# Banded attention stage rewritten, with the norm before it and the norm and gate after it moved inside

## The chip, the cores and the metric

One Trainium2 chip, one core. The metric is the device time of one execution in microseconds (us), median of the runs. The profile is of one execution of its own.

## The reference, cut to what matters

The model is attention A, an expert mixture, banded attention B, an expert mixture, each behind a layer norm and added to x (8 x 512 x 256, fp32). The change touches only this part:

```python
# x: (8, 512, 256)
x = x + attn_b(layernorm(x))          # 16 heads of 64, window 128, causal
h = layernorm(x)                      # goes on to the second mixture
scores = softmax(h @ gate_w.T)        # 16 experts
# attn_b:
q, k = rmsnorm(x @ wq.T) * q_gamma, rmsnorm(x @ wk.T) * k_gamma   # over all 1024 channels
v = x @ wv.T
s = q @ k.T / 8 + slope_h * (j - i);  s = -1e9 where j > i or j < i - 128
return (softmax(s) @ v) @ wo.T
```

## The kernel before

`hybrid_block` (L2439) runs stages one after the other; each ends on all engines before the next starts. Three stages stand where the change is made:

- `norm_stage` "n2" (L125): per batch of 512 tokens it loads x2, takes mean and variance (L373, L377, L379), POOL raises to the power -1/2 (L349), DVE normalizes (L387), PE transposes (L278), ACT copies (L324), and SP writes the transposed rows `xnT` to DRAM.
- `window_stage` "b" (L1217): 32 tiles of 128 tokens (NT = 4 per batch, B = 8). It reads `xnT` back and writes x3 = x2 + attention.
- `norm_stage` "n3": the same norm on x3, which also writes `xn` and `xnT`, and the gate: logits on PE (L290), softmax over 16 experts into `scores` (L395 to L400).

Inside `window_stage` one round does the attention of tile (b, t), the projections of the next tile and the output projection of the tile before. `WINDOW_ORDER` (L1205) is the order written out by hand that PE and DVE follow; ACT follows nearly the same (`WINDOW_SCALAR_ORDER`). Its steps:

- **Sections** share the one PSUM bank `ps_w`, and each waits until the one before is emptied. `q`, `k`, `v` (two halves each, L1403): six matmuls, 512 wide, with both operands split in a high and a rest part (fp32r, three products for two chunks of channels). q and k are emptied in two steps: ACT squares the bank with a running sum (L1482), then DVE multiplies it by gamma (L1553). v, `q_T`, `k_T` (transposes, L1410) and `out_T` (transposes of the attention output, L1415) are emptied by ACT copies. `out` (L1418): eight plain fp32 matmuls with `woT`, each of which PE runs as two instructions (so do all fp32 matmuls here that are no transposes), then the addition to x (L1560).
- `scores` k (0 to 3): four heads on PE, 64 rows each, two side by side (L1443); DVE adds the bias and takes the row's extreme (L1583); ACT takes exp with the row's sum (L1510).
- `probs_T` k (0 to 7): two heads' probabilities transposed (four transposes, L1452), copied by DVE (L1590).
- `values` k (0 to 7): two heads, the transposed probabilities as weights and v, 64 wide, moving (L1462). After four of them DVE divides by the row sums (L1595, L1596).

POOL does only the power for q and k (L1526) and the product with it (L1529). A tile with t = 0 has no band to its left, so its scores are 128 wide and its transposes and values are half as many. Batches 1 to 6 are a hardware loop (`Fori`, five ways back), the rest is written out. Before the first round DVE alone splits the weights (L445 to L447), in the same order of work as the emptying of the first sections.

Of the kernel before, what the change touches and what calls it, by code (L numbers as in the profile page):

```python
# [14 lines left out]
F32R = mybir.dt.float32r  # L15
# [1177 lines left out]
def scores_later(order, lags):  # L1193

    out = [x for x in order if x[0] != "scores"]
    for k, lag in enumerate(lags):
        place = sum(x[0] != "scores" for x in order[:order.index(("scores", k))]) + lag
        out.insert(min(place, len(order) - len(lags)) + k, ("scores", k))
    return out

WINDOW_ORDER = [  # L1205
    ("out_T", 0), ("scores", 0), ("out_T", 1), ("scores", 1), ("out", 0), ("probs_T", 0), ("probs_T", 1), ("q", 0),
    ("scores", 2), ("q", 1), ("values", 0), ("probs_T", 2), ("values", 1), ("probs_T", 3), ("k", 0),
    ("scores", 3), ("k", 1), ("values", 2), ("probs_T", 4), ("v", 0), ("values", 3), ("q_T", 0), ("probs_T", 5),
    ("q_T", 1), ("values", 4), ("probs_T", 6), ("values", 5), ("k_T", 0), ("probs_T", 7), ("values", 6), ("k_T", 1),
    ("values", 7), ("v", 1),  # L1210
]
WINDOW_SCALAR_ORDER = scores_later(WINDOW_ORDER, (1, 4, 4, 6))
NEXT = ("q", "k", "v", "q_T", "k_T")
PAST = ("out_T", "out")


def window_stage(nc, tag, const, x_d, xnT_d, wqT_d, wkT_d, wvT_d, woT_d, gamma_d, bias_d, y_d):  # L1217
# [9 lines left out]
    HW = BC // HALVES  # L1227
    with ExitStack() as ctx:
# [3 lines left out]
        woT = s.sb("woT", [P, CH, C])  # L1232
        gamma = s.sb("gamma", [P, 2, BC])
        bias = s.sb("bias", [P, BH, 2 * P])
        minus_half = s.sb("minus_half", [P, 2])
        xT = s.sb("xT", [P, 2, KC, P])
        xs = [s.sb(f"x_{part}", [P, 2, KC, P], F32R) for part in ("high", "rest")]
        masked = s.sb("masked", [P, HW])
        x = s.sb("x", [P, 2, C])
# [13 lines left out]
        score = s.sb("score", [P, 4, 2 * P])  # L1253
        low = s.sb("low", [P, 4])
        prob = s.sb("prob", [P, 4, 2 * P])
# [3 lines left out]
        o = s.sb("o", [P, 2, BC])  # L1259
        oT = s.sb("oT", [P, CH, P])  # L1260
# [5 lines left out]
        early_in = s.sem("early_in")  # L1266
        late_in = s.sem("late_in")
        xT_in = [s.sem(f"xT_in{p}") for p in range(2)]
        x_in = [s.sem(f"x_in{p}") for p in range(2)]
        y_out = [s.sem(f"y_out{p}") for p in range(2)]  # L1270
        chain = s.sem("chain")
        held = s.sem("held")
        half_set = s.sem("half_set")
        w_split = s.sem("w_split")
        x_split = s.sem("x_split")
        filled = s.sem("filled")
        emptied = s.sem("emptied")
        squared = s.sem("squared")
        ms_ready = s.sem("ms_ready")
# [4 lines left out]
        exped = s.sem("exped")  # L1284
        transposed = s.sem("transposed")
        copied = s.sem("copied")
        valued = s.sem("valued")
        o_taken = s.sem("o_taken")
        block = ctx.enter_context(s.programs())

        PROLOGUE = 10
        UNIT = 13

        def sections_before(b, t):
            return PROLOGUE if isinstance(b, int) and b == 0 and t == 0 else UNIT * (NT * b + t) + PROLOGUE - 3

        def steps(b, t, first, last, order=WINDOW_ORDER):

            n = sections_before(b, t)
            for kind, k in order:  # L1300
                if (kind in NEXT and last) or (kind in PAST and first):
                    continue
                yield kind, k, n
                if kind in NEXT or kind in PAST:
                    n = n + 1

        def units(engine, unit):

            for t in range(NT):
                unit(0, t, t == 0, False)  # L1310
            with engine.Fori(1, B - 1) as b:
                for t in range(NT):
                    unit(b, t, False, False)
            for t in range(NT):
                unit(B - 1, t, False, t == NT - 1)

        def following(b, t):
            return (b, t + 1) if t < NT - 1 else (b + 1, 0)

        def preceding(b, t):  # L1320
            return (b, t - 1) if t else (b - 1, NT - 1)

        def section_number(b, t, kind, k):

            early = isinstance(b, int) and b == 0 and t < 2
            place = [x for x in WINDOW_ORDER if x[0] in NEXT or (x[0] in PAST and not early)].index((kind, k))
            return place if early and t == 0 else sections_before(*preceding(b, t)) + place

        def first_tile():
            n = 0  # L1330
            for kind, k in WINDOW_ORDER:
                if kind in NEXT:
                    yield kind, k, n
                    n += 1

        def last_tile():
            n = sections_before(B - 1, NT - 1) + UNIT - PROLOGUE
            for kind, k in (("out_T", 0), ("out_T", 1), ("out", 0)):
                yield kind, k, n
                n += 1  # L1340

        def uses(b, t):

            return 2 * b + t // 2 + 1

        @block.sync
        def _(sp):
            def load_xT(b, t):
                sp.dma_start(xT[:, t % 2, :, :], xnT_d[ds(b, 1)].rearrange("a p k t -> p (a k) t")[:, :, t * P:(t + 1) * P]).then_inc(xT_in[t % 2], 16)

# [3 lines left out]
            def store(b, t, done):  # L1354

                hold(sp, emptied, done + 1, held)
                sp.dma_start(tokens(y_d, b, t), x[:, t % 2, :]).then_inc(y_out[t % 2], 16)

            def unit(b, t, first, last):
                static = isinstance(b, int)  # L1360

                if not (static and b == B - 1 and t >= 2):
                    hold(sp, emptied, sections_before(b, t), held)
                    load_xT(b + (t + 2) // NT, (t + 2) % NT)

                if not (static and b == 0 and t < 2):
                    past = (b, t - 2) if t >= 2 else (b - 1, t + 2)
                    store(*past, sections_before(*following(*past)) + 2)
                    hold(sp, y_out[t % 2], 16 * (uses(b, t) - 1), held)
                sp.dma_start(x[:, t % 2, :], tokens(x_d, b, t)).then_inc(x_in[t % 2], 16)  # L1370

            load_xT(0, 0)
            for tile, dram, sem in ((w_whole["q"], wqT_d, w_in["q"]), (ident, const["ident"], early_in), (gamma, gamma_d, early_in),
                                    (w_whole["k"], wkT_d, w_in["k"]), (w_whole["v"], wvT_d, w_in["v"]), (bias, bias_d, late_in), (woT, woT_d, late_in)):
                sp.dma_start(tile[tuple(slice(None) for _ in tile.shape)], dram).then_inc(sem, 16)
            load_xT(0, 1)
            units(nc.sync, unit)
            store(B - 1, NT - 2, sections_before(B - 1, NT - 1) + 2)
# [1219 lines left out]
```

## Time and profile before

| | |
|---|---|
| median of 3 runs | 4155.57 us (4155.28 to 4165.5) |
| the profiled execution, its own time | 4160.83 us |
| its span, first to last instruction | 4158.8 us |
| busy in the span | PE 88%, DVE 59%, ACT 44%, POOL 19% |
| mean granted TensorE clock | 0.946 |
| this part of the span | "n2" from 2118.7, "b" from 2168.9, "n3" 3285.4 to 3348.5 |

A busy PE is not PE at its peak: its matmuls overlap, so the distance from start to start tells their cost. A granted clock of 1.00 is 2.4 GHz, 0.50 is 1.2 GHz.

### The profile page before, as it was taken

Reading aid. Unit: us, or ns where it says so; the run is one execution under the profiler, and the core shown is the slowest. Engines: PE = TensorE matmul, PEld = TensorE weight load, DVE = VectorE, ACT = ScalarE, POOL = GpSimd, SP = SyncE. Lnnn points to the kernel's source line nnn. Section 1 sums busy time; section 2 is a strip of 40 time slices with the busy share of each in tenths; the row PEclk is TensorE's granted clock in tenths of the full one; section 3 lists DMA queues with packets and bytes.
Section 4 is the critical chain, followed back from the end, with each engine's and each line's share of the span. In section 5 each row is a group of like instructions: output and inputs, shape, how many; then the busy total and the mean of one; then the engine's idle time right before and its main releaser. Section 6 shows DMA issues by size and latency. Waiting matters only on the chain. (4 is left out here: it accounts for less than half of the span.)

```text
span 4158.8 us, 91975 instructions
## 1 busy us (share of the span) xinstructions
PE 3639.6 (88%) x33000; PEld 2872.0 (69%) x33000; DVE 2451.2 (59%) x5269; ACT 1842.3 (44%) x3752; POOL 780.7 (19%) x714
## 2 busy tenths in 40 slices
PE   4899999999966969999947899888989787899998
PEld 3566666666655858888835777777777676788887
DVE  4566666666645666666544545444545566666664
ACT  1466666666622324444413444444444232344443
POOL 0122222222210013333210000000000000233332
PEclk9999999999987979999969999999999788899999
DMA  4565556555534234333240000000000232343432
GB/s 178 145 172 170 174 172 173 168 171 174 169 123 150 86 119 122 110 108 117 75 142 33 13 13 12 13 13 13 13 13 15 87 118 93 117 122 111 115 110 44
DMA packets 383709, 424.97 MB, mean 102 GB/s; under 512 B 172864, under 2 KB 323008, under 8 KB 369728
## 3 DMA queue, kind: packets, MB, share of 16 engines
q1 hardware_dynamic: 358720, 386.04, 29.2%
q0 software_dynamic: 24576, 33.57, 4.6%
q8 instruction: 241, 3.95, 0.4%
q14 instruction: 172, 1.41, 0.1%
HBM read 269.24 MB, written 150.27 MB: 101 GB/s over the span
## 5 line engine op out<-in xcount | busy, mean ns | idle before, releaser
L2212 ACT ACTIVATE a_prob<-a_ps_s,a_low 128x512 f32<-128x512 f32 x512 | 318.9, 689 | 48.5 <-DVE a_low L2404 47.5
L2073 PE MATMUL a_ps_p<-a_ident,a_prob 128*128 128x128 f32 x2048 | 311.0, 285 | 14.9 <-ACT a_band L2192 9.0
L2404 DVE TENSOR_REDUCE a_low<-a_ps_s 128x2 f32<-128x1024 f32 x256 | 313.5, 1224 | 8.8
L2264 POOL TENSOR_TENSOR a_below<-a_probT,a_upper 128x512 f32<-128x512 f32 x128 | 164.3, 1284 | 726.4 <-ACT a_probT L2188 371.2
L2073 PEld LDWEIGHTS a_ps_p<-a_ident,a_prob 128*128 128x128 f32 x2048 | 217.7, 141 | 108.6 <-issue 83.3
L2188 ACT COPY a_probT<-a_ps_p 128x512 f32<-128x512 f32 x352 | 194.0, 588 | 155.6 <-PE a_ps_p L2073 155.6
L1510 ACT ACTIVATE b_prob<-b_score,b_low 128x256 f32<-128x256 f32 (+1 forms) x512 | 240.6, 473 | 23.7 <-PE b_ps_p L1452 23.7
L1462 PEld LDWEIGHTS b_ps_o<-b_v,b_probT 128*128 128x128 f32 x1792 | 227.2, 191 | 9.9 <-issue 0.9
L1583 DVE CUSTOM_DVE_ANT_0 b_score<-b_ps_s,b_bias 128x256 f32<-128x256 f32 (+1 forms) x512 | 186.0, 389 | 75.2 <-PE b_ps_s L1443 47.6
L1462 PE MATMUL b_ps_o<-b_v,b_probT 128*128 128x64 f32 x1792 | 228.2, 267 | 0.7 <-DVE b_o L1596 0.7
L2403 DVE TENSOR_TENSOR a_ps_s<-a_ps_s,a_win 128x320 f32<-128x320 f32 (+1 forms) x256 | 135.0, 527 | 140.2 <-PE a_ps_s L2106 135.7
L1590 DVE COPY b_probT<-b_ps_p 128x512 f32<-128x512 f32 (+1 forms) x256 | 155.7, 621 | 101.5 <-PE b_ps_p L1452 97.4
L1482 ACT ACTIVATE b_square<-b_ps_w 128x512 f32<-128x512 f32 x128 | 76.4, 597 | 298.5 <-PE b_ps_w L1403 298.5
L1526 POOL TENSOR_TENSOR b_rrms<-b_ms,b_minus_half 128x2 f32<-128x2 f32 x32 | 22.6, 707 | 972.5 <-DVE b_ms L1556 972.5
L490 ACT ACTIVATE ge_gelu<-ge_ps_g 128x512 f32<-128x512 f32 x128 | 76.5, 598 | 286.6 <-PE ge_ps_u L469 286.6
L490 ACT ACTIVATE fe_gelu<-fe_ps_g 128x512 f32<-128x512 f32 x128 | 76.5, 598 | 285.8 <-PE fe_ps_u L469 285.8
L903 POOL DMA_INDIRECT x<-fe_eo,fe_index_scatter x64 | 121.2, 1894 | 361.2 <-DVE fe_eo L1098 346.6
L903 POOL DMA_INDIRECT out<-ge_eo,ge_index_scatter x64 | 120.0, 1875 | 361.2 <-DVE ge_eo L1098 346.6
L1553 DVE TENSOR_TENSOR b_raw<-b_ps_w,b_gamma 128x512 f32<-128x512 f32 x128 | 88.5, 691 | 164.5 <-ACT b_square L1482 164.3
L506 DVE TENSOR_TENSOR ge_raw<-ge_gelu,ge_ps_u 128x512 f32<-128x512 f32 x128 | 87.8, 686 | 157.0 <-ACT ge_gelu L490 146.0
L506 DVE TENSOR_TENSOR fe_raw<-fe_gelu,fe_ps_u 128x512 f32<-128x512 f32 x128 | 87.9, 686 | 156.8 <-ACT fe_gelu L490 145.5
L278 PE MATMUL n_ps_xT<-n_ident,n_xn 128*128 128x128 f32 x256 | 62.8, 427 | 124.0 <-DVE n_xn L387 124.0
(398 smaller groups left out, 10512.2 us busy)
## 6 DMA issues: line engine op xcount, KB each, us to landing
a_win<-band SPq DMA_DIRECT2D x128, 384.0 KB, 4.8
prob<-a_prob SPq DMA_DIRECT2D x128, 384.0 KB, 3.6
xnT<-n_xnT SPq DMA_DIRECT2D x32, 512.0 KB, 3.0
shift<-a_gbias SPq DMA_DIRECT2D x64, 256.0 KB, 2.4
a_shifted<-shift SPq DMA_DIRECT2D x256, 64.0 KB, 2.0
a_bins<-prob SPq DMA_DIRECT2D x128, 128.0 KB, 3.5
fe_gT<-in_WgT SPq DMA_DIRECT2D x16, 1024.0 KB
fe_uT<-in_WuT SPq DMA_DIRECT2D x16, 1024.0 KB
```

The costliest lines, as they stand in the source:

```text
L490: nc.scalar.activation(gelu[:, slot % 2, :], ps_g[slot % 2][:, :], ACT.Gelu).then_inc(gelu_ready, 1)
L506: nc.vector.tensor_tensor(raw[:, slot % 2, :], gelu[:, slot % 2, :], ps_u[slot % 2][:, :], ALU.mult).then_inc(h_ready, 1)
L903: nc.gpsimd.indirect_dma_start(rows_y, bass.IndirectOffsetOnAxis(index[1][:, q, t:t + 1], 0), eo[:, q, t, :], None, bounds_check=B * T - 1 ...
L1462: mm = nc.tensor.matmul(ps_o[:, h % 8 * BD:(h % 8 + 1) * BD], probT[:, k % 2, r, c, :], v[:, t - 1 + c, h * BD:(h + 1) * BD], start=(c == ...
L1510: nc.scalar.activation(prob[:, hh, lo * P:], score[:, hh, lo * P:], ACT.Exp, bias=low[:, hh:hh + 1], scale=-1.0, accum_out=rsum[:, t % 2, ...
L1583: nc.vector.tensor_tensor_reduce(out=score[:, hh, lo * P:], in0=ps_s[k % 2][hh % 2][:, hh // 2, lo * P:], in1=bias[:, h, lo * P:], scale=- ...
L1590: nc.vector.tensor_copy(probT[:, k % 2, :, lo:, :], ps_p[k % 2][:, :, lo:, :]).then_inc(copied, 1)
L2073: last = nc.tensor.transpose(bank[:, c * P:(c + 1) * P], prob[:, t % 2, h, 32 + c * P:32 + (c + 1) * P], ident[:, :])
L2188: last = nc.scalar.copy(probT[:, t % 2, h, :], ps_p[i][:, :])
L2212: nc.scalar.activation(prob[:, t % 2, h, 32:32 + T], ps_s[pair][:, r, :], ACT.Exp, bias=low[:, h:h + 1]).then_inc(exped, 1)
L2264: nc.gpsimd.tensor_tensor(below[:, t % 2, :, :], probT[:, t % 2, :, t * P:(t + 1) * P], upper[:, :].unsqueeze(1).to_broadcast([P, HG, P]), ...
L2404: nc.vector.reduce_max(low[:, 2 * pair:2 * pair + 2], both[:, :, :], AX.X, negate=True).then_inc(maxed, 1)
```

## The change

The two calls of `norm_stage` around it go, and `window_stage` is written anew:

- Every engine has its own written order, and each step names its tile by an offset from the round's (0: attention, 1: projections, 2 and 3: norm and load ahead, -1 and -2: output, second norm, gate). The rounds are (-1,2) to (8,1), 36 in all; the hardware loop is now batches 2 to 6.
- The norm in front: x is loaded once, in natural layout, and kept; DVE normalizes, PE transposes in a section `x`, ACT makes the high part from the bank, DVE the rest. The norm behind: DVE on the sum in SBUF, POOL the power, PE a section `xn_T`, ACT a copy, two stores for each tile; the gate is a section of each batch's last tile.
- q and k are emptied by one DVE copy, ACT squares the copy in SBUF; q and k gamma are multiplied into one vector of gains, applied by DVE as it empties `q_T`.
- The probabilities are divided before they are transposed: a reciprocal for two heads on DVE, the product on POOL (`divide`, in place, 128x512).
- `values` swaps its operands: v is the weights (64 columns), the transposed probabilities move (128 wide), and the two heads go to partitions 0 to 63 and 64 to 127 of `ps_o`. So the output comes out transposed and `out_T` goes; ACT and DVE split it into a high and a rest part, and `out` becomes 24 fp32r matmuls 256 wide.
- Score and probability buffers hold 8 heads instead of 4. One semaphore for each kind of section replaces the count of all of them.
- The weights' high parts are made by ACT, the rests by DVE; woT is split too.

```diff
-WINDOW_ORDER = [
-    ("out_T", 0), ("scores", 0), ("out_T", 1), ("scores", 1), ("out", 0), ("probs_T", 0), ("probs_T", 1), ("q", 0),
...
+WINDOW_ORDER = [
+    ("scores", 0, 0), ("x", 0, 1), ("scores", 1, 0), ("out", 0, -1), ("probs_T", 0, 0), ("q", 0, 1), ("scores", 2, 0), ("q", 1, 1),
+    ("probs_T", 1, 0), ("values", 0, 0), ("k", 0, 1), ("scores", 3, 0), ("k", 1, 1), ("probs_T", 2, 0), ("values", 1, 0), ("xn_T", 0, -1),
+    ("probs_T", 3, 0), ("v", 0, 1), ("values", 2, 0), ("gate", 0, -1), ("probs_T", 4, 0), ("q_T", 0, 1), ("values", 3, 0), ("probs_T", 5, 0),
+    ("q_T", 1, 1), ("probs_T", 6, 0), ("values", 4, 0), ("k_T", 0, 1), ("values", 5, 0), ("probs_T", 7, 0), ("k_T", 1, 1), ("values", 6, 0),
+    ("values", 7, 0), ("v", 1, 1),
+]
+WINDOW_VECTOR_ORDER = [
+    ("probs_T", 6, -1), ("probs_T", 7, -1), ("rest", 1, -1), ("biased", 0, 0), ("x", 0, 1), ("biased", 1, 0), ("inverse", 0, 0), ("biased", 2, 0),
...
+    ("probs_T", 2, 0), ("biased", 6, 0), ("mean", 0, 1), ("probs_T", 3, 0), ("biased", 7, 0), ("inverse", 5, 0), ("gate", 0, -1),
+    ("inverse", 6, 0), ("probs_T", 4, 0), ("q_T", 0, 1), ("inverse", 7, 0), ("rest", 0, 0), ("q_T", 1, 1), ("probs_T", 5, 0),
+]
+WINDOW_POOL_ORDER = [
+    ("divide", 0, 0), ("divide", 1, 0), ("divide", 2, 0), ("x_pow", 0, 2), ("y_pow", 0, -1), ("divide", 3, 0), ("divide", 4, 0), ("pow", 0, 1),
+    ("normed", 0, 1), ("divide", 5, 0), ("divide", 6, 0), ("normed", 1, 1), ("divide", 7, 0),
+]
...
+                        for c in range(lo, 2):
+                            for r in range(2):
+                                h = 2 * k + r
+                                mm = nc.tensor.matmul(ps_o[BD * r:BD * r + BD, k % 4 * P:(k % 4 + 1) * P], v[:, at[1] - 1 + c, h * BD:(h + 1) * BD],
+                                                      probT[:, k % 2, r, c, :], start=(c == lo), stop=(c == 1), skip_group_check=True)
...
+                    elif kind == "divide":
+                        reach_alone(pool, rinv_ready, 8 * w + k + 1)
+                        part = prob[:, 2 * (k % 4):2 * (k % 4) + 2, lo * P:]
+                        by_row = rinv[:, p, 2 * k:2 * k + 2].unsqueeze(2).to_broadcast([P, 2, (2 - lo) * P])
+                        nc.gpsimd.tensor_tensor(part, part, by_row, ALU.mult).then_inc(divided, 1)
...
-        norm_stage(nc, "n2", ident, x2, xnT)
...
-        norm_stage(nc, "n3", ident, x3, xnT, xn_d=xn, gate=ins["gateT"], scores=scores)
+        window_stage(nc, "b", ins, x2, ins["b_wqT"], ins["b_wkT"], ins["b_wvT"], ins["b_woT"], ins["b_gamma"], ins["b_bias"], x3, post=(xn, xnT, ins["gateT"], scores))
```

`reach_alone` is a wait followed by an increment of a spare semaphore on the same engine.

## Rows read from the trace of the kernel before

**Rows 1.** Windows: us; busy PE, PEld, DVE, ACT, POOL; clock, DMA share, GB/s.
```profile
2118.70:2168.90 50.20, 15.72 (x64) 12.55 (x64) 26.31 (x104) 9.37 (x16) 8.21 (x10) 0.50 0.50 169
2168.90:2216.30 47.40, 16.73 (x52) 10.59 (x53) 21.36 (x45) 5.68 (x13) 2.97 (x4) 0.68 0.40 162
2216.30:3285.40 1069.10, 953.78 (x6093) 772.62 (x6092) 527.24 (x1719) 474.60 (x1524) 90.50 (x94) 0.97 0.04 13
3285.40:3348.50 63.10, 44.09 (x192) 40.34 (x192) 34.56 (x144) 11.42 (x24) 8.15 (x9) 0.51 0.61 201
2498.80:2597.10 98.30, 90.09 (x584) 73.16 (x585) 52.10 (x163) 45.84 (x144) 8.75 (x9) 1.00 0.04 13
2597.10:2635.50 38.40, 31.62 (x186) 25.30 (x184) 14.49 (x55) 13.95 (x48) 2.92 (x3) 0.87 0.05 13
```

**Rows 2.** POOL's timeline: start, duration; one of these a round.
```profile
2564.97 0.71 POOL L1526 TENSOR_TENSOR b_rrms<-b_ms,b_minus_half 128x2 f32<-128x2 f32 x1 [29.85 <-DVE b_ms L1556]
2598.02 0.70 POOL L1526 TENSOR_TENSOR b_rrms<-b_ms,b_minus_half 128x2 f32<-128x2 f32 x1 [29.85 <-DVE b_ms L1556]
...
2636.45 0.70 POOL L1526 TENSOR_TENSOR b_rrms<-b_ms,b_minus_half 128x2 f32<-128x2 f32 x1 [35.24 <-DVE b_ms L1556]
...
3144.25 0.71 POOL L1526 TENSOR_TENSOR b_rrms<-b_ms,b_minus_half 128x2 f32<-128x2 f32 x1 [29.80 <-DVE b_ms L1556]
...
3175.66 0.70 POOL L1526 TENSOR_TENSOR b_rrms<-b_ms,b_minus_half 128x2 f32<-128x2 f32 x1 [28.21 <-DVE b_ms L1556]
```

**Rows 3.** PE's timeline in rounds at full clock: start, duration, merged count.
```profile
2565.71 0.40 PE L1403 MATMUL b_ps_w<-b_wv_high,b_x_high 128*128 128x512 f32 x1
2565.94 0.39 PE L1403 MATMUL b_ps_w<-b_wv_rest,b_x_high 128*128 128x512 f32 x1
...
2577.02 1.13 PE L1443 MATMUL b_ps_s<-b_kT,b_qT 64*128 64x256 f32 x8
2578.08 0.66 PE L1415 MATMUL b_ps_w<-b_ident,b_o 128*128 128x128 f32 x4
...
2579.73 3.72 PE L1418 MATMUL b_ps_w<-b_woT,b_oT 128*128 128x256 f32 x16
...
2588.91 1.00 PE L1462 MATMUL b_ps_o<-b_v,b_probT 128*128 128x64 f32 x8
2589.74 0.61 PE L1452 MATMUL b_ps_p<-b_ident,b_prob 128*128 128x128 f32 x4
2590.19 1.00 PE L1462 MATMUL b_ps_o<-b_v,b_probT 128*128 128x64 f32 x8
```

**Rows 4.** PE's timeline in attention A, whose values use 32 columns each.
```profile
602.85 1.08 PE L2115 MATMUL a_ps_o<-a_probT,a_v 128*32 128x128 f32 x32
603.86 0.66 PE L2073 MATMUL a_ps_p<-a_ident,a_prob 128*128 128x128 f32 x4
604.45 0.42 PE L2122 MATMUL a_ps_o<-a_below,a_v_step 128*32 128x128 f32 x8
604.81 0.66 PE L2073 MATMUL a_ps_p<-a_ident,a_prob 128*128 128x128 f32 x4
```

**Rows 5.** Groups by form, 2498.8 to 2597.1: busy, mean ns, idle before.
```profile
L1590 DVE COPY b_probT<-b_ps_p 128x512 f32<-128x512 f32 x20 | 13.5, 687 | 7.3 <-PE b_ps_p L1452 6.7
L1482 ACT ACTIVATE b_square<-b_ps_w 128x512 f32<-128x512 f32 x12 | 7.2, 597 | 23.7 <-PE b_ps_w L1403 23.7
L1529 POOL TENSOR_SCALAR b_normed<-b_raw,b_rrms 128x1024 f32<-128x1024 f32 x6 | 6.6, 1118 | 0.8 <-POOL b_rrms L1526 0.8
```

**Rows 6.** The page's groups: a POOL product of the size of the new one.
```profile
L2264 POOL TENSOR_TENSOR a_below<-a_probT,a_upper 128x512 f32<-128x512 f32 x128 | 164.3, 1284 | 726.4 <-ACT a_probT L2188 371.2
```

**Rows 7.** Timelines: DVE's first emptying; PE at the loop's way back.
```profile
2193.64 0.69 DVE L1553 TENSOR_TENSOR b_raw<-b_ps_w,b_gamma 128x512 f32<-128x512 f32 x1 [0.25 <-DVE b_wv_rest L447]
...
2611.28 1.11 PE L1415 MATMUL b_ps_w<-b_ident,b_o 128*128 128x128 f32 x4 [2.48 <-issue]
```

**Rows 8.** Groups by form of DVE, 2104 to 2165: the norm.
```profile
L387 DVE TENSOR_SCALAR n_xn<-n_x,n_mv,n_rstd 128x256 f32<-128x256 f32 x32 | 11.0, 407 | 10.2 <-POOL n_rstd L349 10.2
```

More of the change, by code:

```diff
@@ L1227, in window_stage @@
     HW = BC // HALVES
+    SECTIONS = ("x", "q", "k", "v", "q_T", "k_T", "out", "xn_T", "gate")
     with ExitStack() as ctx:
@@ L1287, in window_stage @@
         valued = s.sem("valued")
+        o_high = s.sem("o_high")
         o_taken = s.sem("o_taken")
-        block = ctx.enter_context(s.programs())
[L1291 to L1305, printed above, removed]
@@ L1323, in section_number @@
[L1323 to L1340, printed above, removed]
@@ new lines, in window_stage, with tile_at, exists, steps @@
+        gate_exped = s.sem("gate_exped")
+        total_step = s.sem("total_step")
+        gated = s.sem("gated")
+        block = ctx.enter_context(s.programs())
+        def tile_at(b, t, off):
+            return b + (t + off) // NT, (t + off) % NT
+        def exists(kind, b, t):
+            if kind in ("gate", "gate_exp", "gate_end") and t != NT - 1:
+                return False
+            return not isinstance(b, int) or 0 <= b < B
+        def steps(order, b, t):
+            for kind, k, off in order:
+                at = tile_at(b, t, off)
+                if exists(kind, *at):
+                    yield kind, k, *at
@@ new lines, in rounds, with number @@
+        def rounds(engine, unit):
+            for t in range(NT - 2, NT):
+                unit(-1, t)
+            for b in range(2):
+                for t in range(NT):
+                    unit(b, t)
+            with engine.Fori(2, B - 1) as b:
+                for t in range(NT):
+                    unit(b, t)
+            for t in range(NT):
+                unit(B - 1, t)
+            for t in range(2):
+                unit(B, t)
+        def number(b, t):
+            return NT * b + t
@@ new lines, in section @@
+            def section(kind, k, b, t):
+                w = number(b, t)
+                if kind == "x":
+                    pe.wait_ge(x_normed, w + 1)
+                    for c in range(KC):
+                        last = nc.tensor.transpose(ps_w[:, c * P:(c + 1) * P], xn[:, t % 2, c * P:(c + 1) * P], ident[:, :])
+                    last.then_inc(filled["x"], 1)
+                elif kind in ("q", "k", "v"):
+                    pe.wait_ge(x_split, w + 1)
+                    if isinstance(w, int) and w == 0 and k == 0:
```

631 lines of the change are left out of this document (391 added, 240 removed).

## The prediction, made before the change was run

> **What bounds it now.** I read the windows by stage first. The three stages at stake take 50.2 + 47.4 + 1069.1 + 63.1 = 1229.8 us of the profiled span [rows 1]. In the two norm stages no engine is full: PE is busy for 15.7 of 50.2 us in the first and runs at a granted clock of 0.50 (1.2 GHz), so these 113.3 us are latency, a load, a norm, a transpose and a store after one another. In the rounds PE is the engine to look at: in 98.3 us of whole rounds it is busy for 90.1, DVE for 52.1, ACT for 45.8, POOL for 8.8, at a clock of 1.00 [rows 1].
>
> Then the length of a round, from the one POOL power that each has [rows 2]. A full round (t = 1 to 3) takes 2598.02 - 2564.97 = 33.05 us. The one with t = 0 takes 3175.66 - 3144.25 = 31.4 us where the code is written out, and 2636.45 - 2598.02 = 38.4 us at the loop's way back, thus 7.0 us more. There PE stands still for 2.5 us with nothing that the profile shows as its cause [rows 7], and its clock is 0.87 over that round [rows 1]. So 24 x 33.05 + 8 x 31.4 + 5 x 7.0 = 1079.4 us, and 47.4 + 1069.1 - 1079.4 = 37.1 us are the two ends (loads and weights before, the last tile after).
>
> What PE needs in a full round comes from its starts [rows 3]. A 512 wide section instruction is 0.23 us after the one before: six sections of six, 8.3 us. Four transposes 0.45: eight `probs_T` 3.6, four of q and k 1.8, two `out_T` 0.9. `values` 0.84 each: 6.7. `out` 3.72, of which 0.2 overlap with what follows: 3.5. `scores` 1.06 from its start to the next, and 0.14 before it, since four transposes ahead of a group of another array shape take 0.59 and not 0.45 [rows 3, 4]: 4 x 1.20 = 4.8. Sum 29.6, so PE waits 3.4 us in a round, mostly for the single bank of the sections: q and k are emptied by ACT (0.60) and then by DVE [rows 5], one after the other.
>
> **The parts.** *The two norm stages* go: -113.3 us. Their work moves into the rounds: on DVE some 2.3 us a round (statistics, mean, variance and a 0.41 us product, twice [rows 8]), on PE two times two transposes, 0.4 us, and on POOL two powers of at most 0.7.
>
> *PE in a full round.* Sections 8.3, q and k transposes 1.8, `probs_T` 3.6 and `scores` 4.8 stay. `out_T` goes. `out` becomes 24 instructions 256 wide with split operands; half of the 0.23 us of a 512 wide one is 0.115: 2.8 us. The gate is 16 instructions every fourth round, estimated 0.4 a round. `values` is the part in doubt. 128 wide fp32 instructions on 32 columns each take (1.01 - 0.36) / 24 = 0.027 us apiece in attention A, with four side by side, beside 0.15 us that a group costs at its end and 0.14 at its beginning [rows 4]. So one alone would be 0.107, two side by side 0.054; eight are 0.43, plus 0.30 for the two changes of array shape: 0.73 a group, 5.8 a round. The bounds: 0.43 without the changes, 0.86 + 0.30 = 1.16 if the two halves do not run side by side. I take 0.73, as attention A shows both effects on the same form. The Trainium skill (TensorEngine Tiling (Array Packing), Key Properties) says that a change of tiling mode drains TensorE; the trace agrees (the 0.30). By its speedup table alone, 2x for 64 columns, a group would be 0.43 and the round 2.4 us shorter. Sum: 8.3 + 1.8 + 3.6 + 4.8 + 2.8 + 0.4 + 0.4 + 5.8 = 27.9 us, 1.7 less than now.
>
> *What PE waits for.* A bank is now free one DVE copy (0.69) after its section, and the square, on SBUF, is off this path. I walked through the written order with the rows' durations and 0.05 to 0.17 us for each hand-over. From `scores` 0 at zero: `out` 2.6 to 5.3; q starts 0.65 late, after DVE's addition; the second halves of q and k find the bank free, since `scores` between them covers the copy, and k ends at 15.1; v starts 0.6 late, for ACT's copy of `xn_T`. Then the power's chain: the mean of q and k at 17.3, and from there POOL alone does power, q, `divide` 5, `divide` 6, k, `divide` 7: 0.71 + 2 x 1.12 + 3 x 1.28 [rows 2, 5, 6], with 0.28 before each of six (0.8 us of idle in three rounds, [rows 5]): 8.5 us, done at 25.8. `probs_T` 7 waits for it some 0.5 us, and behind it stand 0.45 + 0.44 + 1.46 + 1.4 us of PE: the round ends at 29.6. PE's own sum with its waits, 27.9 + 1.7, ends at the same place. The gate waits for v's copy and holds the bank: 0.7 on average over four rounds. Full round: **30.3 us** (33.05 now).
>
> With t = 0 `scores`, `values` and `probs_T` are half as wide: PE's sum is 22.9 us by the same prices. Waits weigh more, because the short `scores` no longer cover a copy of the bank. Before, the same sum was 23.0 and the waits 8.4; the shorter emptying takes about half of them: **27 us** (31.4 now).
>
> *DVE* gets the norms (2.3), eight reciprocals in place of two (1.2), q_T twice (1.4) and 0.3 of gate, and is rid of two steps of the x split (0.6): 52.1 / 98.3 x 33.05 = 17.5 becomes 22 us of 30. Not the bound, though its waits are in order. *ACT* stays near 15. *POOL* goes from 2.9 to some 14.5 busy. *SP* issues four DMAs a round where it issued three, at 0.4 to 0.6 us each: hidden.
>
> *The loop's way back*: four times, not five, at 7.0: -7.0. I see no reason for another price; between 3 and 10 us each it moves the sum by 16 us either way.
>
> *The ends.* DVE alone splits the weights now and empties its first section only at 2193.64, 24.8 us into the stage [rows 7]. With ACT and DVE in parallel this is some 7 us earlier. Against it: the norm of the first tile (5 us), and behind the last the addition, norm, transpose, gate and two stores (7 us). I leave the ends at 37, with 10 us either way.
>
> **Sum.** 24 x 30.3 + 8 x 27 + 4 x 7.0 + 37.1 = 727.2 + 216 + 28 + 37.1 = 1008.3 us, against 1229.8: -221.5. The profiled execution took 4160.83, so 3939.3; it stands 5.3 us above the median of the runs shown, so against that median **3934 us**, 5.3% faster.
>
> **Rivals.**
> *A, PE comes close to its own sum.* The written order leaves PE hardly a wait, POOL's hand-overs are shorter than 0.28 us, full rounds take 28.6 and short ones 25.6: 24 x 1.7 + 8 x 1.4 = 52 us less, 3882. For it: one DVE copy per section. Against: POOL's serial 8.5 us sit in the second half of the round.
> *B, the two halves of `values` do not pair*, 8 x 0.43 = 3.4 us a full round and half of that in a short one, 96 us: 4030. Against it: four column groups do pair in attention A [rows 4]; for it: there are two instructions to each product here, and v, 64 columns, has to be loaded each time. DVE's many small waits in order could cost the same: 1 us more in each round is 32 us, 3966.
> *C, POOL and DVE get in each other's way.* POOL is now busy half of the time beside DVE. If each of the two SBUF to SBUF products of the norms waits for a `divide`, DVE loses up to 2 x 1.28 us a round, some 80 us: 4014. The Trainium skill (SBUF — State Buffer, Practical consequences) says that a DVE instruction in a two-port mode, or with two SBUF inputs, and a GpSimd one block each other for their whole length. The norm's product takes 407 ns for 256 elements [rows 8], no less for each element than the copy out of PSUM with its 687 ns for 512 [rows 5], so it is not in such a mode; the bias step reads PSUM.
> *D, slower than before: TensorE's clock.* If the gaps on PE make it fall to 1.2 GHz in the rounds, as in the norm stages (0.50 with PE busy for a third) and partly at the way back (0.87) [rows 1], PE's 27.9 us become about 50, so a round is 22 us longer. From ten such rounds of 32 on, the 221 us are gone; in all of them it would be 4155 + 480, some 4640. Against it: rounds in which PE waits a tenth keep 1.00 [rows 1], and the new ones wait for less.
> *E, no change.* The stages are gone from the program by the diff, so only a loss of 7 us a round could hide it. Nothing in the rows is of that size.
>
> **Chances.** Forecast (full rounds of 29.3 to 31.3) 0.5; A 0.2; B or DVE's waits 0.17; C 0.07; D 0.04; E 0.02. The range takes in A and B: 3870 to 4030. 0.3% is 12 us, about what a measurement of this kernel can tell from no change; faster by more 0.95, within it 0.01, slower 0.04.
>
> **What would show it.** The stage from its first DMA to the next stage's first takes about 1008 us. The distance of POOL's powers of q and k is 30.3 us in full rounds. A group of `values` takes 0.73 us from start to start, `out` 2.8, a `divide` 1.28. PE's wait before `probs_T` 7 is for POOL, before the first q for DVE. Wrong would be: `values` at 1.16 (B), products of the norm much over 0.41 us (C), a clock under 0.9 in rounds away from the way back (D), PE waiting mostly for DVE (its order, not POOL, sets the round).

## The result: 3917.7 us, and the profile after

The changed kernel takes 3917.7 us (median of 4, 3910.7 to 3919.1), the kernel before 4155.4: a ratio of 0.942 (95% interval 0.940 to 0.944), 5.7% faster. Forecast were 3934 us and a range of 3870 to 4030.

Below are the windows of the changed kernel: its attention stage from SP's first DMA to the first of the next stage, then two full written-out rounds, then one batch of the hardware loop (columns as in [rows 1]).

```profile
2107.88:3101.30 993.42, 911.39 (x6408) 668.23 (x6408) 624.79 (x2202) 484.01 (x1561) 364.49 (x417) 0.96 0.08 25
2197.51:2254.20 56.69, 56.48 (x417) 41.95 (x416) 39.74 (x135) 30.14 (x98) 24.44 (x27) 1.00 0.07 20
2484.32:2604.97 120.65, 112.81 (x801) 82.83 (x800) 76.77 (x274) 59.56 (x194) 45.56 (x53) 0.99 0.06 19
```

The stage takes 993.4 us; the three stages that it replaces took 1229.8 [rows 1]. That is 236.4 us less, and the medians differ by 237.7. The stage before all this, which the change doesn't touch, ends between 2107.9 and 2121.1 us in the executions of this study. So kernels are compared here by the length of this stage and by the distance of POOL's powers, not by a single span.

POOL's powers give the rounds, as in [rows 2]:

```profile
2225.87 0.70 POOL L1658 TENSOR_TENSOR b_rrms<-b_ms,b_minus_half 128x2 f32<-128x2 f32 x1 [3.32 <-DVE b_ms L1716]
2254.20 0.70 POOL L1658 TENSOR_TENSOR b_rrms<-b_ms,b_minus_half 128x2 f32<-128x2 f32 x1 [3.29 <-DVE b_ms L1716]
2281.27 0.70 POOL L1658 TENSOR_TENSOR b_rrms<-b_ms,b_minus_half 128x2 f32<-128x2 f32 x1 [3.74 <-DVE b_ms L1716]
2311.23 0.70 POOL L1658 TENSOR_TENSOR b_rrms<-b_ms,b_minus_half 128x2 f32<-128x2 f32 x1 [3.29 <-DVE b_ms L1716]
```

A full round without a gate takes 28.33 us (33.05 before), the short one 27.07 (31.4), the next one, which has the gate, 29.96. In the windows PE is busy for 56.48 of the 56.69 us of two full rounds, DVE for 39.74.

The time from the stage's start to its first power fell to 32.2 us, and from the last power to the end it is 45.4; before, they were 36.6 and 44.8. So the 236.4 us are 113.3 for the two norm stages, 119.3 for the 31 distances between powers, and 3.8 at the ends.

Full rounds repeat within 0.1 us from kernel to kernel where nothing changes them; the stage does not. Three of the kernels below (values head by head, both heads in one half, all written out) do the same work up to the first power and take 33.6 to 34.3 us to it, where the changed kernel takes 32.2; the rounds with a gate differ too. So a difference of a few us in the stage, the 3.8 at the ends included, says little by itself.

**Where PE's time goes.** PE's timeline in a full round (start, duration):

```profile
2227.17 0.66 PE L1567 MATMUL b_ps_o<-b_probT,b_v 128*64 128x128 f32 x8
2227.75 0.66 PE L1556 MATMUL b_ps_p<-b_ident,b_prob 128*128 128x128 f32 x4
2228.25 0.62 PE L1490 MATMUL b_ps_w<-b_ident,b_normed 128*128 128x128 f32 x4
2228.80 0.66 PE L1567 MATMUL b_ps_o<-b_probT,b_v 128*64 128x128 f32 x8
2229.39 0.66 PE L1556 MATMUL b_ps_p<-b_ident,b_prob 128*128 128x128 f32 x4
2229.88 0.60 PE L1490 MATMUL b_ps_w<-b_ident,b_normed 128*128 128x128 f32 x4
```

`values` takes 0.59 us from its start to the next (2228.80 to 2229.39), and the transposes before it 0.10 more than the usual 0.45 (2228.25 to 2228.80). No wait is marked here; in the whole round PE's idle time adds up to 0.11 us, 0.08 of it before the first q. POOL beside it, after the power at 2225.87:

```profile
2226.97 1.12 POOL L1664 TENSOR_SCALAR b_normed<-b_raw,b_rrms 128x1024 f32<-128x1024 f32 x1 [0.40 <-POOL b_rrms L1658]
2228.05 2.04 POOL L1669 TENSOR_TENSOR b_prob<-b_prob,b_rinv 128x512 f32<-128x512 f32 x2
2230.07 1.12 POOL L1664 TENSOR_SCALAR b_normed<-b_raw,b_rrms 128x1024 f32<-128x1024 f32 x1
2231.16 1.04 POOL L1669 TENSOR_TENSOR b_prob<-b_prob,b_rinv 128x512 f32<-128x512 f32 x1
```

Power, q, two products, k and the last product are over in 6.3 us, not 8.5: one product takes 1.02 us, and only the power is followed by a gap (0.40). Yet the first of these matters: q's product ends at 2228.09, and PE's transposes of q start at 2228.25. PE is full and at the same time starts this step only 0.16 us after what it needs is there. Which of the two sets the round, PE's work or the chain through POOL, is what the experiments ask.

### The profile page after: what moved, and what is told of

It is laid out like the page before. It is cut to its first block and busy times, and to the rows that moved or that the text cites. A ratio compares the mean times of both kernels' runs of the same rounds, so it can differ in the third digit from the quotient of the medians.

```text
span 3908.9 us, 92834 instructions
## 1 busy us (share of the span) xinstructions
PE 3506.8 (90%) x33008; PEld 2695.1 (69%) x33008; DVE 2466.3 (63%) x5459; ACT 1826.1 (47%) x3736; POOL 1036.2 (27%) x1016
## 5 line engine op out<-in xcount | busy, mean ns | idle before, releaser
L1669 POOL TENSOR_TENSOR b_prob<-b_prob,b_rinv 128x512 f32<-128x512 f32 (+1 forms) x256 | 238.3, 935 | 386.5 <-DVE b_rinv L1730 386.3
L1725 DVE CUSTOM_DVE_ANT_0 b_score<-b_ps_s,b_bias 128x256 f32<-128x256 f32 (+1 forms) x512 | 178.1, 385 | 74.9 <-PE b_ps_s L1548 71.6
L1567 PE MATMUL b_ps_o<-b_probT,b_v 128*64 128x128 f32 x1792 | 150.3, 288 | 4.4 <-DVE b_probT L1734 3.8
L1556 PE MATMUL b_ps_p<-b_ident,b_prob 128*128 128x128 f32 x896 | 148.3, 283 | 5.8 <-POOL b_prob L1669 5.8
L479 PE MATMUL fe_ps_d<-fe_d_rest,fe_h_high 128*128 128x256 f32 x512 | 144.4, 282 | 9.8 <-DVE fe_eo L1098 6.9
L479 PE MATMUL ge_ps_d<-ge_d_rest,ge_h_high 128*128 128x256 f32 x512 | 144.3, 282 | 9.8 <-DVE ge_eo L1098 6.9
L2568 DVE COPY a_probT<-a_ps_p 128x512 f32<-128x512 f32 x160 | 110.4, 691 | 64.7 <-PE a_ps_p L2254 62.1
```

What stands on the lines that cost most here:

```text
L479: last = nc.tensor.matmul(ps_d[t // 2][:, t % 2, :], h[b][:, slot, t * P:(t + 1) * P], d[a][:, j, :], start=(j == 0 and t % 2 == 0 and (a, ...
L1669: nc.gpsimd.tensor_tensor(part, part, by_row, ALU.mult).then_inc(divided, 1)
L1725: nc.vector.tensor_tensor_reduce(out=score[:, h % 8, lo * P:], in0=ps_s[k // 2 % 2][r][:, k % 2, lo * P:], in1=bias[:, h, lo * P:], scale= ...
```

## Experiments

Each is the changed kernel with one edit, except where two are named or the text says so. "Full round" is the mean distance of powers over the two full rounds of the first batch, written out; "stage" is from its first DMA to that of the next stage. Both come from one profiled execution for each kernel.

| kernel | full round, us | stage, us |
|---|---|---|
| changed kernel | 28.35 | 993.4 |
| values head by head | 28.40 | 996.9 |
| both heads in one half of the columns | 31.75 | 1069.5 |
| `out` with 8 of 24 products | 27.26 | 984.3 |
| first half of v with 2 of 6 products | 28.34 | 990.2 |
| the same, mean ahead of a bias step | 28.09 | 994.2 |
| one more product on POOL | 29.34 | 1015.8 |
| no `divide` | 28.36 | 990.4 |
| k normed on ScalarE | 28.63 | 994.4 |
| q and k emptied in two steps | 30.63 | 1069.5 |
| second norm and gate behind | 28.32 | 959.4 + 62.9 |
| all written out | 28.35 | 969.4 |
| all written out, k's transposes moved | 28.70 | 981.0 |

### PE work outside and beside the chain

```diff
# out
-  terms = [... for o_part, w_part in ((1, 0), (0, 0), (0, 1))]
+  terms = [... for o_part, w_part in ((0, 0),)]
# the first half of v
+  if (kind, k) == ("v", 0):
+      terms = [(c, 0, 0) for c in range(KC)]
```

> Leaves out the two rest products of the output projection: 8 of 24 matmuls are left (high by high). They are at the head of a round, before the chain from q and k over the pow begins. 16 x 0.118 = 1.9 us of TensorE work less per round. Theory 1 (TensorE's sum, or anything that stands in line behind TensorE's work at the head of the round): -1.9 x 32 = -60 us, the stage at 933 to 945 us. Theory 2 (VectorE's work of about 20 us per round or ScalarE's sets the rounds): the stage within 10 us of 993.

> Leaves out the two rest products of the first half of v: 2 of its 6 matmuls are left, 4 x 0.234 = 0.94 us less TensorE work per round, and this work stands beside the chain mean, pow, normed q, divide 5 and 6, normed k, divide 7 on POOL. Theory 1 (TensorE's own sum alone sets the rounds): -0.94 x 32 = -30 us, the stage at 963 us. Theory 2 (POOL's chain from the pow to the seventh divide is as long as TensorE's work beside it; in the changed kernel's timeline the transposes of q start only 0.2 us after the product that they read has ended, 2228.09 to 2228.25, and those of k 0.3 us): only 0.2 to 0.4 us per round come off, -6 to -12 us, and TensorE shows new waits for b_normed or b_prob.

Taking 0.94 us of v away gave nothing in a full round. PE waits at the transposes of q for POOL instead (timeline of that kernel):

```profile
2242.44 0.63 PE L1492 MATMUL b_ps_w<-b_ident,b_normed 128*128 128x128 f32 x4 [0.76 <-POOL b_normed L1666]
```

Taking 1.9 us away from `out` gave 1.09 a full round, which lies between the two theories. The rest became a wait for a `divide` at the head of the round:

```profile
2242.22 0.66 PE L1556 MATMUL b_ps_p<-b_ident,b_prob 128*128 128x128 f32 x4 [0.76 <-POOL b_prob L1669]
```

The stage gained only 9 us, within the 10 of theory 2, but not for its reason. The fifteen rounds with t = 2 or 3 gained 15.8; those with t = 0 or 1 (the gate of the batch before is in the latter) took 7.2 more. At the four ways back the granted clock is 0.86 to 0.90 here and 0.95 to 1.00 in the changed kernel.

### POOL longer, POOL shorter

```diff
  pool.wait_ge(ms_ready, w + 1)
+ nc.gpsimd.tensor_tensor(idle[:, :], idle[:, :], idle[:, :], ALU.mult).then_inc(idled, 1)
+ pool.wait_ge(half_set, 1)
  nc.gpsimd.tensor_tensor(rrms[:, :], ms[:, :], minus_half[:, :], ALU.pow).then_inc(pow_ready, 1)
# and in another kernel
- nc.gpsimd.tensor_tensor(part, part, by_row, ALU.mult).then_inc(divided, 1)
+ pool.sem_inc(divided, 1)
```

> One more product of POOL on a scratch tile (128x512, about 1.04 us, as a divide) before the pow of each round; nothing is left out. Theory 1 (POOL has slack behind TensorE): the stage stays at 993 us within 3. Theory 2 (the chain from the pow has 0.2 to 0.3 us of slack): +0.8 us per round, +25 us; the stage at 1015 to 1022 us, TensorE waiting for b_normed.

> Leaves out POOL's products with the reciprocals: the probabilities stay unnormalized, and POOL keeps the pow, the two normed products and the powers of the norms. The runs so far say that full written-out rounds of 28.34 us are not set by TensorE's sum (0.94 us less TensorE work beside the chain: 28.33; one 1.04 us product more ahead of the pow: 29.33). Theory 1 (the chain over POOL sets them: pow 0.70, gap 0.4, normed q 1.12, divides 5 and 6 2 x 1.02, normed k 1.09, divide 7 1.04): the chain to the transposes of k is 2.0 us shorter and that to the last probabilities 3.1 us; full rounds at 26.2 to 27.3 us, then bound by TensorE or by the next chain; the stage 35 to 65 us shorter. Theory 2 (another cycle that also holds the pow, but not the divides): rounds stay at 28.3. For the norms: if VectorE's 128x256 products wait for POOL's divides, their medians return from 0.78 and 0.86 us to the 0.41 of before.

One product more ahead of the power costs 0.99 us a full round, nearly its own length (1.00 us from its start to the power's), and PE waits 0.83 for q:

```profile
2246.34 0.63 PE L1492 MATMUL b_ps_w<-b_ident,b_normed 128*128 128x128 f32 x4 [0.83 <-POOL b_normed L1670]
```

But all eight `divide` gone, with k's product 2.0 us sooner, gives nothing. So the chain is tight only as far as q's product. The distance from the power to PE's transposes of q says the same: it is 2.38 us in the changed kernel (2225.87 to 2228.25), where no wait is marked, and 2.37 in the kernels with one product more and with less of v, where PE visibly waits. What stands behind it on POOL, the part on which my forecast laid the 0.5 us before `probs_T` 7, is covered.

> The normed product of k moves from POOL to ScalarE (behind its last exp of the round, where it has about 0.8 us of idle time and then 2 us more); POOL's chain behind the pow is normed q and divides 5, 6 and 7. Nothing is left out. Theory 1 (POOL's chain sets the round): divide 7 and normed k are ready 1.1 us sooner; full rounds from 28.34 to about 27.3 to 27.6 us, the stage 20 to 30 us shorter. Theory 2 (the chain is tight only as far as normed q): rounds stay at 28.3 within 0.1.

```diff
# POOL's order
-  ("divide", 5, 0), ("divide", 6, 0), ("normed", 1, 1), ("divide", 7, 0),
+  ("divide", 5, 0), ("divide", 6, 0), ("divide", 7, 0),
# ScalarE's order
-  ("exp", 7, 0), ("high", 0, 0),
+  ("exp", 7, 0), ("normed", 1, 1), ("high", 0, 0),
...
# POOL, ahead of the power
+  reach_alone(pool, k_normed, w)
# ScalarE
+  nc.scalar.activation(normed[:, 1, :], raw[:, 1, :], ACT.Copy, scale=rrms[:, 1:2]).then_inc(k_normed, 1)
```

Theory 2 was right that there is no gain; the round even takes 0.3 us more. Two side effects of the edit make up nearly all of it. The power waits for one semaphore more and starts 0.20 us behind the mean and not 0.08. And ScalarE's high part of the output now stands behind k's product, so that VectorE waits longer for it (the first line; the changed kernel below it), and the next `values` comes 0.13 us later behind its transposes:

```profile
2240.80 0.69 DVE L453 TENSOR_TENSOR b_oT_rest<-b_ps_o,b_oT_high 128x512 fp32r<-128x512 f32 x1 [0.59 <-ACT b_oT_high L1618]
```

```profile
2230.12 0.69 DVE L453 TENSOR_TENSOR b_oT_rest<-b_ps_o,b_oT_high 128x512 fp32r<-128x512 f32 x1 [0.32 <-ACT b_oT_high L1613]
```

### Both limits at once

> Leaves out the two rest products of the first half of v (as the run before, whose full rounds stayed at 28.33 us, stage 990.2), and VectorE's mean of the squares goes ahead of its subtraction of the bias of heads 12 and 13, behind which it started 0.43 us after its squares were there (ACT's last read of the accumulator ends 2225.20, b_ms starts 2225.63). Theory 1 (TensorE's sum, and the chain emptying of k, square, mean, pow, normed q, transposes of q together with the TensorE work outside it, are of equal length to within 0.1 us; so neither cut alone gives anything): both cuts together give 0.25 to 0.4 us per full round, 27.95 to 28.1, the stage 6 to 12 us shorter than 990.2. Theory 2 (something else holds the round): 28.33 stays.

```diff
-  ("probs_T", 2, 0), ("biased", 6, 0), ("mean", 0, 1), ("probs_T", 3, 0),
+  ("probs_T", 2, 0), ("mean", 0, 1), ("biased", 6, 0), ("probs_T", 3, 0),
```

Full rounds of 28.09 us, 0.25 less, where v's cut alone gave nothing; PE's wait for q fell from 0.76 to 0.48. So a loop of dependences holds the full round at 28.35: emptying of k, square, mean, power, q's product, then all of PE's work from q's transposes to the end of the next k. The cut in v lies outside it, the move of the mean and the longer POOL inside. That PE's own sum is as long is read from its 0.11 us of idle time in the changed kernel; the move of the mean alone, with v whole, which would show it by a gain of no more than that, was not run.

The stage didn't follow: 994.2 us, against my 978 to 984. Against the changed kernel its fifteen rounds with t = 2 or 3 gained 4.2 us, but those with t = 0 or 1 took 2.4 more and its start and first round 2.4 more. More on these rounds with the second norm.

### Do the two heads run side by side?

```diff
# head by head
-  for c in range(lo, 2):
-      for r in range(2):
+  for r in range(2):
+      for c in range(lo, 2):
# one half for both heads
-  ps_o[BD * r:BD * r + BD, k % 4 * P:(k % 4 + 1) * P]
+  j = h % 8
+  ps_o[BD * (j // 4):BD * (j // 4) + BD, j % 4 * P:(j % 4 + 1) * P]
```

> The changed kernel with the values products of a pair of heads issued head by head (both key blocks of one head, then both of the other) and not key block by key block, so that the two heads' 64-column products stand side by side only at the change of head. Stage of 993.4 us in the changed kernel's profile. Theory 1 (TensorE's own sum sets the rounds, and the alternation of the two column halves is what made a values group 0.67 us and not 0.84 as before): a group goes back towards 0.84 us, 24 rounds x 8 groups x 0.17 = +33 us if no pair overlaps, about +20 if the products at the change of head still do; the stage takes 1010 to 1030 us. Theory 2 (POOL's chain or VectorE sets the rounds): groups longer, the stage within 5 us of 993. Theory 3 (the alternation did nothing, the group is shorter for another reason): neither group nor stage moves.

> The changed kernel with both heads of a values group written to the same 64 columns' half of TensorE's array (heads 0 to 3 of a half of o to the lower, 4 to 7 to the upper half), so that no two products of a group can stand side by side; as many products, of the same sizes. Computes something else: the heads reach the output projection in another order. Issuing the same pairs head by head had left the group at 0.59 us from start to start, against my expectation. Theory 1 (two heads in different halves of the columns do run side by side, whatever their order within the group): without it a group of 4 products takes longer by about as much as the overlap gave; a group of before, whose products of 64 columns could not overlap, took 0.84 us, so 0.84 to 1.0 us and, with all eight groups on TensorE's sum, 8 x 0.2 to 0.4 = +1.6 to +3 us per full round, the stage +45 to +90 us. Theory 2 (nothing ran side by side, and the group is shorter because its products are of another shape): the group stays at 0.59 and the stage within 3 us of 993.4.

Head by head changed nothing: the group stays at 0.59. That looked as if nothing ran side by side. With both heads in one half it takes 1.01 (2242.67 to 2243.68):

```profile
2242.67 1.09 PE L1568 MATMUL b_ps_o<-b_probT,b_v 128*64 128x128 f32 x8
2243.68 0.66 PE L1556 MATMUL b_ps_p<-b_ident,b_prob 128*128 128x128 f32 x4
```

The same products in the same number cost 0.42 us more a group, 8 x 0.42 = 3.4, and the full round grew by 3.4; the sums of PE's other groups over the round agree within 0.05 us. So the halves do run side by side, and within a group of four products the order of issue is of no matter.

### The bank emptied in one step

```diff
# ScalarE
-  act.wait_ge(raw_taken, 4 * w + qk_number(kind, k) + 1)
-  nc.scalar.activation(square[:, :], raw[:, which, k * HW:(k + 1) * HW], ACT.Square, ...
+  act.wait_ge(filled["qk"], 4 * w + qk_number(kind, k) + 1)
+  nc.scalar.activation(square[:, :], ps_w[:, :], ACT.Square, ...
# VectorE
-  dve.wait_ge(filled["qk"], 4 * w + qk_number(kind, k) + 1)
+  dve.wait_ge(squared, 4 * w + qk_number(kind, k) + 1)
```

In ScalarE's order, the first q also stands one exp earlier.

> Undoes one part of the change: q and k are again squared by ScalarE in PSUM first, and VectorE copies them only then, so that the shared PSUM tile of TensorE's sections is emptied in two steps that follow each other (ScalarE about 0.7 us, VectorE 0.66 us), four times in a round. Nothing is left out. Theory 1 (this takes TensorE's time at q and k, which stand ahead of the pow in the chain that sets the round): 1.0 to 2.0 us per round, +30 to +60 us on the stage. Theory 2 (the other sections between two of q and k cover the longer emptying): within 5 us of 993.

It costs 2.28 us a full round and 76 us on the stage, above what I expected. PE's waits in one round of it:

```profile
2271.88 0.51 PE L1483 MATMUL b_ps_w<-b_wq_high,b_x_rest 128*128 128x512 f32 x1 [0.44 <-DVE b_raw L1705]
2275.06 0.50 PE L1483 MATMUL b_ps_w<-b_wk_high,b_x_rest 128*128 128x512 f32 x1 [0.48 <-DVE b_raw L1705]
2278.22 0.50 PE L1483 MATMUL b_ps_w<-b_wk_high,b_x_rest 128*128 128x512 f32 x1 [0.44 <-DVE b_raw L1705]
2281.39 0.44 PE L1504 MATMUL b_ps_w<-b_ident,b_yn 128*128 128x128 f32 x2 [0.48 <-DVE b_raw L1705]
```

Four waits, 1.84 of the 2.28 us; the other 0.44 are not marked as waits. Undone in the new order, this small part of the change is worth about a third of the whole gain.

### The second norm, and the clock

> Undoes one part: the second norm, its transposes and the gate come out of the rounds and run as the separate stage of before, behind attention. Nothing is left out. Theory 1 (the stage of its own took 63.1 us before, and inside the rounds this work costs little, since VectorE and ScalarE have idle time there; TensorE loses 0.27 + 0.12 us per round, and the gate of a batch about 1.5 us in one round of four): attention at 993 minus 15 to 30 us, plus 63 us, the two together 1026 to 1042 us. Theory 2 (the inside norm hides completely): attention 993, together 1056 us. Theory 3 (the norm's VectorE work, lengthened by POOL's products, is on the chain): attention shorter by 50 us or more, and the merging of this norm gained nothing.

```diff
-  ("xn_T", 0, -1), ... ("gate", 0, -1), ... ("y_stats", 0, -1), ... ("y_pow", 0, -1), ... ("store_normed", 0, -1)
...
+  norm_stage(nc, "n3", ident, x3, xnT, xn_d=xn, gate=ins["gateT"], scores=scores)
```

Attention took 959.4 us, the stage behind it 62.9: together 28.9 us more than inside. Attention is 34.0 us shorter without this work, more than I had allowed. It is not the full rounds (28.32): there PE only waits for q instead.

```profile
2239.15 0.63 PE L1487 MATMUL b_ps_w<-b_ident,b_normed 128*128 128x128 f32 x4 [0.35 <-POOL b_normed L1661]
```

It is the rounds with t = 1, which hold the gate (20.0 us), those with t = 0 (7.3) and the end behind the last power (8.6), while its start and first round take 3.8 us more. The first gate round is 27.52 us without the gate and 29.96 with it, 2.4 us for 16 products that alone take 1.96 (`b_gwT`, 2283.53 in the changed kernel).

The gate round also shows how the clock scatters. The same round of batch 1, with the same code, in the changed kernel and in the written-out one (windows; the clock is the third number from the end):

```profile
2281.27:2311.23 29.96, 28.83 (x193) 20.77 (x194) 19.34 (x73) 15.15 (x51) 10.98 (x13) 1.00 0.06 18
```

```profile
2289.09:2320.93 31.84, 31.28 (x193) 22.56 (x194) 19.59 (x73) 15.12 (x51) 11.00 (x13) 0.89 0.06 18
```

PE's same 193 counted instructions take 28.83 us at 1.00 and 31.28 at 0.89, and the round is 1.9 us longer. In all these kernels the clock is below 1.00 only at the two ends of the stage and in rounds with t = 0 or the one after, and it is with t = 0 that PE stands still most: for 1.6 us of the short round's 27.07, and for 5.9 of 33.06 at a way back. In the kernel with the mean moved ahead the first two loop rounds ran at 0.90 and 0.89 (0.95 and 1.00 in the changed one) and took 65.6 us against 63.1; the next two took 61.0 against 63.8. So it is scatter, and no run here controls it.

### The loop's way back

```diff
-  with engine.Fori(2, B - 1) as b:
-      for t in range(NT):
-          unit(b, t)
-  for t in range(NT):
-      unit(B - 1, t)
+  for b in range(2, B):
+      for t in range(NT):
+          unit(b, t)
```

> The hardware loop over batches 2 to 6 is replaced by the same rounds written out; nothing else is changed and nothing left out. A batch took 121.3 to 121.4 us in the loop and 113.8 written out. Theory 1 (the way back and the register waits of the loop cost about 7.5 us a batch): 5 x 7.5 = -37 us, the median near 3880. Theory 2 (written out, the instruction streams of five more batches have to be fetched, and engines wait for code): less than half of it, or slower. Theory 3 (loop batches are slower by their place, DMA traffic and the clock, and not by the loop): within 8 us of 3918.

3895.0 us (3890.4 to 3899.8), a ratio to before of 0.936 (0.934 to 0.938): the fastest kernel of the study, 22.7 us below the changed one, and the stage is 24.0 shorter. That is 4.8 us for each of the five batches, not 7.5: the loop does cost, and longer code eats none of it that can be seen (rounds with t = 0 take 27.05 to 27.08 in every batch, full ones 28.32 to 28.43). By rounds: the four at a way back take 32.8 on average and 27.1 written out, 5.7 less each, and a full round in the loop 28.6 to 28.9 and not 28.35. At the way back in the changed kernel PE shows two stops:

```profile
2493.38 1.25 PE L1567 MATMUL b_ps_o<-b_probT,b_v 128*64 128x128 f32 x16 [1.03 <-DVE b_probT L1734]
2498.38 0.71 PE L1548 MATMUL b_ps_s<-b_kT,b_qT 64*128 64x128 f32 x8 [2.14 <-issue]
```

The second stands where the 2.48 us of [rows 7] stood, and its cause isn't shown here either. The first is new: the copies of `probs_T` 6 and 7 now stand in VectorE's next round, behind its own way back, and VectorE is idle for 2.04 us before them.

> The written-out kernel (stage 969.4 us, median 3895) with one pair of TensorE's sections exchanged: the first transposes of k now go ahead of values 4 and not between values 4 and 5, so that two groups in the halved column layout follow each other. Nothing is left out. Theory 1 (each change of layout costs TensorE 0.1 to 0.2 us, and this stretch is neither covered nor beside the chain over the pow): two changes less, -0.2 to -0.35 us per full round, the stage 5 to 9 us shorter than 969.4. Theory 2 (the changes cost nothing, or the copy of probs_T 6, which must wait for values 4, comes too late for values 6): no gain, or slower by up to 0.5 us a round.

```diff
-  ("probs_T", 6, 0), ("values", 4, 0), ("k_T", 0, 1), ("values", 5, 0),
+  ("probs_T", 6, 0), ("k_T", 0, 1), ("values", 4, 0), ("values", 5, 0),
```

Slower by 0.35 us a full round; 3906.4 us, stage 981.0. That is within theory 2's number, but neither theory had named the cause. The sections share one bank, and the transposes of k now come before VectorE has emptied those of q:

```profile
2241.74 0.66 PE L1488 MATMUL b_ps_w<-b_ident,b_normed 128*128 128x128 f32 x4 [0.55 <-DVE b_qT L1709]
```

## Why the prediction was right, and where it was not

**The sum** was 16 us too high (3934 against 3917.7), and the stage 15 (1008.3 against 993.4). The saving in the norm stages, 113.3, stands as it was. The ends were taken as unchanged and gained 3.8. The rest of the miss is in the rounds: 119.3 us gained where the terms gave 108.2 (24 x 2.75 + 8 x 4.4 + 7.0), 11.1 more.

**PE's own sum** was forecast at 27.9 us with 0.4 for the gate, thus 27.5 without it. The starts of one full round of the changed kernel add up to 28.4: six sections 9.4 (8.3 forecast, because a section's first product takes 0.33 to the next and one ahead of a group of other layout 0.1 more), eight `probs_T` 4.4 (3.6), `scores` 4.3 (4.8), `out` 2.95 (2.8), transposes of q and k 2.1 (1.8), of x and its norm 0.65 (0.4), `values` 4.6 (5.8). The forecast counted each layout change with the tiled group; part of it lies with the neighbours, which is why the one term is too high and the others too low. So PE's sum was 0.8 too low and its waits 1.6 too high, and half of the second error was made good by the first: that the time came out so close is in part luck.

**The step that failed** is "What PE waits for", 1.7 us a round. PE's idle time is 0.11 us a round: 0.08 before the first q and nothing before `probs_T` 7. The hand-overs were priced one by one and added; in the real order each is shorter than the work in front of it, and the one chain that is tight runs to the same length as PE's work. Rival A's mechanism ("the written order leaves PE hardly a wait") is what happened, at 28.35 us and not 28.6, but its time, 3882, was not reached: short rounds take 27.07 and not 25.6, and a gate costs 2.4 us, a way back 5.7, a lower clock some 2. The forecast's 29.3 to 31.3 for full rounds, with the gate's share in it, was wrong: the 23 full rounds between powers average 29.24, 1.06 under the 30.3, and those with t = 2 or 3 take 28.3 to 28.9.

**The short round** was forecast at 27 and takes 27.07, by luck. The sum was 22.9 for PE and 4.1 of waits. Between the two powers the trace has PE busy for 25.44 us, so it waits for 1.6 only, and its work takes 2.5 more than forecast:

```profile
2254.20:2281.27 27.07, 25.44 (x193) 18.80 (x191) 17.12 (x68) 13.46 (x49) 10.08 (x13) 1.00 0.07 21
```

**POOL's chain** was forecast at 8.5 us, and as the partner of PE's sum. It is 6.3, since the product was priced by [rows 6] at 1.28 and takes 1.02, and since five of six hand-overs don't exist. That could be read before: the 0.8 us of idle time in [rows 5] is one gap a round, behind the power, for two products. That PE's sum and a chain through the power end at the same place was right; it is another chain, which ends with q's product and not with the last `divide`. The run without any `divide` shows this, and the run with one product more shows the other half. DVE, forecast at 22 us a round and no bound, is busy for 19.9; POOL, forecast at 14.5, for 12.2.

**`values`** (rival B): forecast 0.73 a group, measured 0.59 plus 0.08 to 0.10 with its neighbour. The two halves do pair; without pairing the stage is 76 us longer. Rival B had put 96 us on that. The price of one instruction was right: 8 x 0.107 and 0.15 for one change of shape give 1.01, 8 x 0.054 and 0.15 give 0.58 (both are estimates from [rows 4]); what was too much is the second 0.15. By the up to 2x that the Trainium skill gives for 64 columns (TensorEngine Tiling (Array Packing), Theoretical Speedup) 1.01 would become 0.51, an estimate; measured is 0.59, with the change of layout in both.

**Rival C, POOL against VectorE.** I had argued from the duration of the norm's product for each element [rows 8, 5] that POOL could not hold it up. It does (tile views; min/median/max in ns), first in the changed kernel, then without `divide`:

```profile
L1695 DVE TENSOR_SCALAR b_xn<-b_x,b_mv,b_rstd x32: 405/777/781, 2113.6 to 3022.2; 128x256 f32<-128x256 f32 x32
L1756 DVE TENSOR_SCALAR b_yn<-b_x,b_y_mv,b_y_rstd x32: 402/857/861, 2193.5 to 3093.4; 128x256 f32<-128x256 f32 x32
```

```profile
L1695 DVE TENSOR_SCALAR b_xn<-b_x,b_mv,b_rstd x32: 405/410/415, 2122.7 to 3032.3; 128x256 f32<-128x256 f32 x32
L1756 DVE TENSOR_SCALAR b_yn<-b_x,b_y_mv,b_y_rstd x32: 396/404/415, 2206.0 to 3101.1; 128x256 f32<-128x256 f32 x32
```

So that step of the reasoning was wrong, and the small price is another matter: 0.37 + 0.45 = 0.82 us a round, and VectorE, busy for 39.7 of 56.7 us, absorbs it. The Trainium skill (SBUF — State Buffer, Practical consequences) says of a VectorE instruction in a two-port mode and a GpSimd one that whichever comes second is fully blocked; the trace agrees that a `divide` lengthens the other, by less than its own 1.02 us, and to which of the page's modes this product belongs no run here shows.

**Way back and clock.** The loop's four ways back were forecast at 4 x 7.0 = 28.0 us; written out, the stage is 24.0 shorter. The rounds at a way back are 5.7 longer each, 22.8, part of which (1.03) is a stop that only the new order has. That the full rounds in the loop are longer too, by 0.8 us a batch, was not in the sum. Rival D, the clock, came in a mild form: 0.96 over the stage, as before (0.97), with single rounds at 0.89 and about 2 us each (32.09 against 30.04 for the same round of two batches).

**The gate** was priced at 1.1 us a round on average, 4.4 us each; it costs 2.4 at full clock (29.96 against 27.52 us).

## What to carry to other kernels

When an engine is full by its busy time, shorten its work at one place and lengthen a suspected partner at another: here a cut of 0.94 us gave nothing and a product of 1.0 us more cost 0.99, which no share of busy time would have told. Look first at how often a shared bank is emptied in two steps; undoing that, with one step of ScalarE's order moved, cost 76 us. And don't add up hand-overs of an order written by hand as if each ended a wait: ask of each what work stands in front of it.

## Not expected of the hardware

- Two fp32 products in different column halves run side by side whether they are issued in turn or head by head (group 0.59 us either way, 1.01 in one half).
- VectorE's product with two scalars for each partition, in SBUF, takes 0.41 us alone and 0.78 to 0.86 beside POOL's products.
- A POOL product of 128x512 takes 1.02 us here with a factor for each row of 256, and also with three plain operands in one tile (2242.97 to 2243.97), where attention A's takes 1.28 [rows 6].
- The same round of the same code took 29.96 us at a granted clock of 1.00 and 31.84 at 0.89 in two executions.
